# Row buffers and the order of work in the expert tiles of the first mixture

## The reference, cut to what matters

```python
final_e = _route(tokens, router_w)          # one expert id per token
for e in range(E):                          # E = 8
    h = jax.nn.relu(tokens @ W1[e] + b1[e]) # 128 -> 512
    y = h @ W2[e] + b2[e]                   # 512 -> 128
    out = out + jnp.where((final_e == e)[:, None], y, 0.0)
```

## Time and profile before

| | us |
|---|---|
| median of three runs | 2063.07 |
| the profiled execution, its own time | 2055.11 |
| its span, from first to last instruction | 2053.4 |
| first gather issued | 610.53 |
| first turn on PE | 613.49 |
| first scatter issued | 621.04 |
| last scatter issued | 752.65 |
| fetch back issued by SP | 754.99 |
| last statistics of the stage on DVE | 771.43 |

### The profile page before, as it was taken

How to read it: one execution, slowest core, us unless ns; L and a number is a source line. 1 busy time by engine, 2 the same in 40 slices (tenths; PEclk the granted TensorE clock), 3 DMA queues, 4 the chain that set the end, 5 groups by cost and what they waited for, 6 DMA issues and landing times. The chain is left out here.

```text
span 2053.4 us, 23725 instructions
## 1 busy us (share of the span) xinstructions
PE 1472.2 (72%) x7090; PEld 822.6 (40%) x7090; DVE 1029.6 (50%) x2652; ACT 755.8 (37%) x1585; POOL 444.8 (22%) x623
## 2 busy tenths in 40 slices
PE   3899999997327644543399966775999227858767
PEld 1233333332216541331166643563566106745422
DVE  4778888884562244986322243334000546631445
ACT  1467777776103314742122213212322320024334
POOL 2334443310015531000154411000000030000036
PEclk6799999999658985876699977766999665658889
DMA  6111111110301120000543300000000000000001
GB/s 122 38 48 49 43 45 48 48 33 29 106 4 37 40 66 6 0 0 1 110 92 86 81 2 4 0 0 21 1 1 1 2 5 1 0 0 11 1 21 31
DMA packets 68375, 63.25 MB, mean 31 GB/s; under 512 B 17055, under 2 KB 55279, under 8 KB 68215
## 3 DMA queue, kind: packets, MB, share of 16 engines
q1 hardware_dynamic: 65703, 56.64, 11.5%
q0 software_dynamic: 2560, 5.25, 1.0%
HBM read 47.63 MB, written 13.79 MB: 30 GB/s over the span
## 5 line engine op out<-in xcount | busy, mean ns | idle before, releaser
L1339 DVE TENSOR_REDUCE a_nm<-a_aps 128x1 f32<-128x512 f32 x512 | 333.5, 686 | 95.1 <-PE a_aps L1109 95.1
L1303 ACT ACTIVATE a_prob<-a_sps 128x512 f32<-128x512 f32 x512 | 271.2, 597 | 116.1 <-PE a_sps L1121 115.1
L1109 PE MATMUL a_aps<-a_K,a_Q 96*128 96x512 bf16 x512 | 195.6, 402 | 26.2 <-DMA a_K<-k_parts 25.9
L1121 PE MATMUL a_sps<-a_Q,a_K 99*128 99x512 bf16 x512 | 156.3, 385 | 1.0 <-ACT a_prob L1303 1.0
L1130 PE MATMUL a_ops<-a_prob,a_Vg 128*32 128x512 f32 x1024 | 137.5, 612 | 0.0
L2049 POOL TENSOR_TENSOR m1e_h<-m1e_a,m1e_t 128x512 f32<-128x512 f32 x72 | 91.1, 1266 | 146.5 <-DVE m1e_t L2066 142.9
L1109 PEld LDWEIGHTS a_aps<-a_K,a_Q 96*128 96x128 bf16 x512 | 50.2, 98 | 154.4 <-DVE a_nm L1339 88.9
L2066 DVE TENSOR_TENSOR m1e_t<-m1e_G,m1e_gps 128x512 f32<-128x512 f32 x64 | 43.9, 688 | 134.0 <-PE m1e_gps L1995 109.7
L2037 ACT ACTIVATE m1e_a<-m1e_hps 128x512 f32<-128x512 f32 x72 | 43.0, 597 | 144.2 <-PE m1e_gps L1995 144.2
L2411 DVE TENSOR_TENSOR x_resid<-x_resid,m2e_yps 128x512 f32<-128x512 f32 x8 | 5.5, 688 | 158.5 <-PE m2e_yps L2361 158.5
L1995 PE MATMUL m1e_gps<-x_normT,m1e_w 128*128 128x512 f32 x144 | 75.5, 607 | 8.0 <-DVE m1e_t L2066 8.0
(11 more groups left out here) (487 smaller groups left out, 2849.3 us busy)
## 6 DMA issues: line engine op xcount, KB each, us to landing
m1e_G<-gates_by_expert SPq DMA_DIRECT2D x16, 1024.0 KB, 10.6
a_Q<-q_parts SPq DMA_DIRECT2D x192, 32.0 KB
q_parts<-a_partsq SPq DMA_DIRECT2D x8, 384.0 KB, 2.8
k_parts<-a_partsk SPq DMA_DIRECT2D x8, 384.0 KB, 2.8
a_K<-k_parts SPq DMA_DIRECT2D x32, 96.0 KB
a_K<-k_parts SPq DMA_DIRECT2D x32, 64.0 KB
m0w_w<-in_L_ffn_W SPq DMA_DIRECT2D x1, 2048.0 KB, 9.1
tokens<-m_nr_xn SPq DMA_DIRECT2D x8, 256.0 KB
```

What stands on the lines that cost most here:

```text
L1109: nc.tensor.matmul(aps[n % 3][:, :], Q[0:MAX, head, q * P:(q + 1) * P], K[0:MAX, head, :], start=True, stop=True).then_inc(a_ready, 1)
L1121: nc.tensor.matmul(sps[(NS * u + k) % 3][:, :], K[0:KB, head, k % TC * P:(k % TC + 1) * P], Q[0:KB, head, :], start=True, stop=True).then_ ...
L1303: nc.scalar.activation(prob[u % 2][:, k // TC, k % TC, :], sps[n % 3][:, :], ACT.Exp).then_inc(p_done, 1)
L1339: nc.vector.tensor_reduce(nm[u % 2][:, s:s + 1], aps[n % 3][:, :], AX.X, ALU.max, negate=True).then_inc(a_used, 1)
```

## The change

It does four things in `tiles_by_expert`. The rows have eight buffers instead of four, and eight semaphores `x_loaded` (NX = 8; `y` keeps four). POOL issues eight gathers first, and then for each t scatter(t) ahead of gather(t+8), where it had gather(t+4) ahead of scatter(t). PE does down(t-1) ahead of turn(t+2). DVE loads each expert number once, for `copy_weights`, and keeps it in a register until `output` of the same tile, two steps of its loop later; before, it loaded it in both.

```diff
-    NB = 4
+    NB, NX = 4, 8
-        x, y = [p.sb(f"x{i}", [P, D]) for i in range(NB)], [p.sb(f"y{i}", [P, D]) for i in range(NB)]
+        x, y = [p.sb(f"x{i}", [P, D]) for i in range(NX)], [p.sb(f"y{i}", [P, D]) for i in range(NB)]
...
             def gather(t):
-                wait(pool, x_turned, t - NB + 1)
-                nc.gpsimd.indirect_dma_start(x[t % NB][:, :], None, xs[:, :],
-                                             bass.IndirectOffsetOnAxis(token[:, t:t + 1], 0)).then_inc(x_loaded[t % NB], 16)
+                wait(pool, x_turned, t - NX + 1)
+                nc.gpsimd.indirect_dma_start(x[t % NX][:, :], None, xs[:, :],
+                                             bass.IndirectOffsetOnAxis(token[:, t:t + 1], 0)).then_inc(x_loaded[t % NX], 16)
...
-            for t in range(NB):
+            for t in range(NX):
                 gather(t)
             for t in range(N):
-                if t + NB < N:
-                    gather(t + NB)
                 scatter(t)
+                if t + NX < N:
+                    gather(t + NX)
...
             for t in range(N + 1):
                 if t < N:
                     up(t)
+                if t >= 1:
+                    down(t - 1)
                 if t + 2 < N:
                     turn(t + 2)
-                if t >= 1:
-                    down(t - 1)
...
-            def copy_weights(t):
-                e = expert(v, t)
+            def copy_weights(t, e):
...
-            def output(t):
-                e = expert(v, t)
+            def output(t, e):
...
-            copy_weights(0)
+            last = this = expert(v, 0)
+            copy_weights(0, this)
             copy_tokens(0)
             for t in range(N):
                 if t + 1 < N:
-                    copy_weights(t + 1)
+                    after = expert(v, t + 1)
+                    copy_weights(t + 1, after)
                     copy_tokens(t + 1)
                 if t >= 1:
-                    output(t - 1)
-            output(N - 1)
+                    output(t - 1, last)
+                last, this = this, after
+            output(N - 1, last)
```

More of the change, by code:

```diff
@@ L1536, in tiles_by_expert @@
         xps, hps, yps = ([p.ps(f"{n}{i}") for i in range(2)] for n in ("xps", "hps", "yps"))
-        x_loaded, y_stored = ([p.sem(f"{n}{i}") for i in range(NB)] for n in ("x_loaded", "y_stored"))
+        x_loaded, y_stored = ([p.sem(f"{n}{i}") for i in range(k)] for n, k in (("x_loaded", NX), ("y_stored", NB)))
         x_turned, xT_done, w_copied = p.sem("x_turned"), p.sem("xT_done"), p.sem("w_copied")
@@ L1581, in turn @@
             def turn(t):
-                pe.wait_ge(x_loaded[t % NB], 16 * (t // NB + 1))
+                pe.wait_ge(x_loaded[t % NX], 16 * (t // NX + 1))
                 wait(pe, xT_done, t - 1)
-                nc.tensor.transpose(xps[t % 2][:, 0:P], x[t % NB][:, :], net.ident[:, :]).then_inc(x_turned, 1)
+                nc.tensor.transpose(xps[t % 2][:, 0:P], x[t % NX][:, :], net.ident[:, :]).then_inc(x_turned, 1)
             def up(t):
```

## The result

The changed kernel took 2044.5 us (median of four runs, 2038.6 to 2046.7) against 2063.35 before: ratio 0.9903, interval 0.9877 to 0.9930. It is faster, by 19 us and not by the 42 forecast; 2044.5 lies outside the range of 2015 to 2040. The profiled execution of after took 2046.15 us, span 2044.4.

What follows compares the result with a forecast made beforehand. Waits in a ring of PE and POOL were taken to bound the tile loop; afterwards POOL would pace at 2.56 us a tile, 42 us less: 2055.1 to 2013, or 2021 from the runs' median 2063.1; range 2015 to 2040.

Steps and rivals of the forecast that it cites:

- POOL's sum: Tile loop: POOL's issues pace it, so the last scatter starts at 710.6 instead of 752.65, 42 us less.
- The open register load: Before PE's down products: 15.9 us idle would go; as rival, PE pays the load every tile, 2040 us, chance 0.14.
- PE's waits for gathered rows: PE's turn in the tile loop: the 28.3 us of waits go, but for 5.2 before the first turn.
- Eighth gather: POOL at the loop's start: the eighth gather starts at 619.5, the first at 610.53.
- The tail: Loop's end, through PE and VectorE: scatter(32) at 702.6, the last scatter at 710.6.
- POOL's pair: POOL in the tile loop: one scatter and one gather with their pauses take 2.56 us a tile.
- Down ahead of the turn: PE's order in the tile loop: cost taken as zero; up to 0.5 us a tile hidden by POOL's pace.
- the ring: PE's turn waits for a gather, issued behind a scatter that waits for PE's down products; 3.37 us a tile.
- One load on VectorE: VectorE in the tile loop: the removed register load stood before a wait, so it saves nothing.
- The copies: Rival: VectorE's weight copies hold up POOL's DMA issues, 14 us over 32 tiles, 2035 us, chance 0.04.
- Not doing what it says: Rival: gathers land late, so eight buffers only move the wait; 2063 us, no change, chance 0.05.
- The slower clock: Rival: PE gets the lower clock throughout the loop, 3.7 us a tile; 13 us slower, 2076 us, chance 0.03.

Runs made afterwards that it cites:

- f1: The changed kernel again, nothing edited, in a second session; loop 101.8 us, 2028.8 us, ratio 0.9822.
- g1: The changed kernel once more, unedited; loop 102.2 us, 2017.3 us, ratio 0.9790.
- k1: The changed kernel, unedited, as a probe of a later session's state; loop 101.8 us, 2019.2 us.
- e4: The changed kernel with the first eight gathers only, so later tiles are computed from old rows; loop 84.6 us, 2008.9 us.
- e3: The kernel before with only the down products put ahead of the next turn, four buffers; loop 109.4 us, 2033.1 us, ratio 0.9850.
- g4: The kernel before with one register load a tile on VectorE, nothing else; loop 142.0 us, 2065.0 us, ratio 1.0018.
- f2: The changed kernel with the second register load a tile on VectorE put back in output; loop 102.4 us, 2021.9 us.
- g2: The kernel before once more, unedited, for its later stages; loop 144.1 us, 2061.6 us, ratio 0.9991; third layer's attention 206.7 us.
- e2: The kernel before with eight row buffers only, gather still ahead of scatter; loop 102.5 us, 2019.7 us, ratio 0.9807.
- h1: The changed kernel again, unedited, in a fourth session; loop 126.8 us, 2045.7 us, ratio 0.9947.
- h2: The kernel before with eight row buffers only, run again in the fourth session; loop 128.1 us, 2039.8 us, ratio 0.9915.
- the fifth session: The changed kernel, the kernels of e3 and e4, and the kernel before, run again in one session; 2019.2 us for the changed kernel.
- f3: The changed kernel with the gather ahead of the scatter on POOL; loop 101.9 us, 2020.1 us.
- g3: The kernel before with the scatter ahead of the gather on POOL, four buffers; loop 294.8 us, 2215.5 us, ratio 1.072.

## Why the prediction was wrong, point by point

**The step that failed is the one that makes POOL's sum the loop's: "So POOL paces the loop, and of its 52.3 idle us most are what is gained".** It takes y to be ready whenever POOL comes to a scatter. In the recorded result it was not: POOL stood 30.5 us in 20 waits for y, because PE's finished products were announced late (the updates of 646.16 to 646.38 above). The loop took 126.9 us, not 100.1. In three other profiles of the same kernel (f1, g1, k1) POOL did pace it, 101.8 to 102.2 us, and the kernel took 2028.8, 2017.3 and 2019.2 us around the forecast 2021. The prediction had no term and no rival for semaphores that come late, and its range ended at 2040.

**Term by term, in the undisturbed profile f1:**
- The open register load goes: yes. Of 15.9 us before the down products 0.2 are left.
- PE's waits for gathered rows go but for the first: no. Of 28.3 us 10.7 are left, in 11 waits, the first of 5.2 among them, and its weight loads stand 12.1 us in 20 waits. The prediction let PE work ahead of POOL and did not ask where that ends: at the gather issued last. The number did not suffer, since POOL paced.
- Eighth gather 9.0 us after the first: 9.00. First scatter 10.3 after it: 10.5. Scatter(32) at 92.1: 92.7.
- The tail was mis-sized. I followed the path over PE and VectorE and found 8.0 us from scatter(32) to the last; POOL's own seven more issues take 7 x 1.28 = 9.0 (702.48 to 711.60 is 9.1). The longer of two paths counts, and I had not worked out the second. Cost: 1 us.
- POOL's pair, 2.56 us: 2.57 (32 pairs from 620.30 to 702.48).
- Down ahead of the turn costs nothing: yes (e4, where POOL does not pace and so can't hide it). But it is no mere reordering either: with four buffers it takes 33 us off the loop by itself (e3). The prediction looked at what it costs and not at what it does to the ring; beside eight buffers there was nothing left for it to gain.
- One load on VectorE: nothing (g4, f2), as said.
- The rest of the kernel neither pays nor gains: within what its stages vary by the clock (g2).

**The rivals.** The open register load: refuted by e4. The copies: a scatter took 0.99 us on average in f1 against 0.985 before; single issues were held up, by up to 0.16 us there (the last section has the rows). Not doing what it says: no, eight buffers alone took 40 us off the loop (e2). The slower clock: the loop's mean rose to 0.95 in f1; in the recorded result it was 0.87, since the late semaphores leave PE idle.

**What is not settled** is why PE's semaphores come late in some sessions. Shown: two of five profiles of the changed kernel have them and three don't; they took hold of the eight-buffer kernel with the old order beside it; the kernel before took 2058.8 us in that session, no more than in others; a chip that had them had been free of them in another session. In the four places of the recorded trace that I followed (readers at 621.0, 630.3, 646.3, 668.7) they arrive together 2.3 us after the start of the last DMA that POOL issued before it stood still (618.7, 628.0, 643.9, 666.4). The trace itself is thinner in such a loop: 832, 843 and 840 semaphore updates recorded (after, h1, h2) in place of 1650. Outside the loop next to none are missing, and most of the missing ones are those of DMAs (of some 1250 in the loop 513 are there in after). All executions of such a session are long, not the profiled one alone: the nine executions of h1 took 2042.9 to 2056.0 us, the ten of f1, g1 and k1 2011.4 to 2031.5. All this could mean that the recording, or whatever carries updates, is overloaded; it was only observed, and no run shows whether the updates would be late without a recording. Whether a loop with pauses (e3), or one without late gathers (e4), would be spared in such a session was to be told by the fifth session, and it did not have the state. No kernel that avoids them was found.

No version beat the others clearly: undisturbed, the change, e2 and f3 all lie at 102 us of loop, because all issue 80 indirect DMAs of 1.28 us through POOL. A faster loop needs fewer of these, as e4 shows from the other side.

## What to carry to other kernels

Write the ring down: add up what lies between the last event that a prefetch waits for and its use, divide by the number of tiles that the order of work puts in between, and compare with each engine's own work per tile. Here 6.6 / 2 = 3.3, 6.7 / 3 = 2.2 and 6.6 / 1 us a tile stand against 3.46, 2.59 (POOL's 2.56 takes over) and 7.65 measured from scatter 0 to scatter 32 in before, e3 and g3; a swap of two lines on PE was worth nearly as much as four more buffers, and one on POOL cost 150 us. And where two engines become nearly full at once, repeat the measurement in another session before reading the mechanism off one trace.

## What the runs showed of the hardware that I had not expected

- PE's semaphore updates reached ACT and DVE up to 4.7 us late, several at once, in some sessions only, while the trace has the products themselves starting in time.
- VectorE's weight copy and POOL's DMA issues hold each other up, by little and only where they meet at certain offsets. In f1 the 17 copies that began 0.64 to 0.70 us after the start of an issue took 0.52 to 0.57 us, and all but one of the others 0.43 (on average 486 ns against 427 before). The other way round, a scatter that began 0.12 us after a copy took 1.15 us, where they take 0.99 on average, and in g1 and e2 a gather that began 0.04 and 0.05 us after one took 1.22 us. In before nearly all copies began 0.17 to 0.20 us after an issue; they took 0.43 us and no scatter more than 1.00, so the place that the prediction looked at could not show it. The rows are f1's:

```profile
656.26 0.99 POOL L1569 DMA_INDIRECT token_outputs<-m0e_y,m0w_target  x1 [0.30 <-issue]
...
656.91 0.56 DVE L1631 COPY m0e_w1s<-m0w_w 128x512 f32 x1 [0.48 <-PE m0e_hps L1591]
...
706.21 0.43 DVE L1631 COPY m0e_w1s<-m0w_w 128x512 f32 x1 [0.47 <-issue]
706.33 1.15 POOL L1569 DMA_INDIRECT token_outputs<-m0e_y,m0w_target  x1 [0.30 <-issue]
```

The Trainium skill (SBUF — State Buffer, the paragraph on the "DVE blocks DMA" trap) has GpSimd locked out while VectorE copies fp32 from SBUF to SBUF; the issue of 706.33 agrees with that, at 0.16 us for this one and 6 ns a scatter on average.
